# A fused LRU and mixture-of-experts layer: more expert tiles inside the last attention quad, loads before stores, third parts on VectorE, and other unused products

## What is computed

```
x = x + LRU(layernorm(x))              # complex linear recurrence, 64 states, input and output matrices, plus D
y = layernorm(x)
h = y + Attention(rmsnorm(y) * ln1)    # 16 heads of size 8, softmax over all 1024 keys
m = rmsnorm(h) * ln2
logits = m @ gate.T                    # 8 experts, the two best, softmax of their logits
out = sum over the 2 experts e: weight_e * (silu(m @ w1[e].T) * (m @ w3[e].T)) @ w2[e].T
result = x + h + out
```

## Time and profile before

| | |
|---|---|
| runs, us | 1098.22, 1098.86, 1103.92; median 1098.86 |
| profiled execution, us | 1099.61, its span 1097.9 |
| busy share of the span | PE 83%, DVE 80%, ACT 64%, POOL 32% |
| mean granted clock of PE | 0.935 |
| opening | 0 to 196.9 us |
| last quad, first tile to last | 881.3 to 918.5 us |
| tiles behind the quad | 922.9 to 1080.6 us |

### The profile page before, as it was taken

One profiled execution on the slowest core, in us unless ns is written; L12 is line 12 of the kernel. 1 busy time (PEld: TensorE's weight loads), 2 busy tenths in 40 slices (PEclk: granted clock), 3 DMA queues, 4 the chain that ended last, 5 costly groups with the idle time before them and its releaser, 6 DMA issues.

```text
span 1097.9 us, 18609 instructions
## 1 busy us (share of the span) xinstructions
PE 909.0 (83%) x5924; PEld 379.2 (35%) x5924; DVE 877.7 (80%) x1585; ACT 698.8 (64%) x1475; POOL 352.1 (32%) x636
## 2 busy tenths in 40 slices
PE   0376754999999999899899999989999888787783
PEld 0254430222222223222222222222332246787772
DVE  4987759899999988889889999888897733674365
ACT  2235530688888887788878888878877765342331
POOL 4001121000000143433522614524465513456563
PEclk9688875999999999999999999999998999898987
DMA  9984445000010110100100010010010111222263
GB/s 320 387 299 111 108 121 137 8 24 8 27 27 8 24 28 11 43 9 28 45 9 23 25 35 23 13 39 22 16 36 9 45 33 41 57 70 71 69 193 110
DMA packets 62943, 74.48 MB, mean 68 GB/s; under 512 B 11264, under 2 KB 41216, under 8 KB 62464
## 3 DMA queue, kind: packets, MB, share of 16 engines
q1 hardware_dynamic: 56048, 63.07, 19.2%
q0 software_dynamic: 4608, 9.58, 2.6%
q10 hardware_dynamic: 2192, 0.66, 0.3%
HBM read 28.09 MB, written 44.79 MB: 66 GB/s over the span
## 4 chain that ended last, share of the span: by engine, by line
PE 59%; DVE 25%; ACT 7%; issue 5%; DMA 2%; another core or an unknown queue 1%; ACTq 1%; DVEq 0%; POOLq 0%; SPq 0%
PE ps L1605 19%; PE ps L1595 14%; DVE smax L1222 12%; PE ps L1546 7%; PE ps L1703 7%; PE ps L1719 3%; ACT prob L987 3%; PE ps L1563 2%; PE ps L1664 2%; DMA wgate<-gate_t 1%; ACTq L867 1%; PE ps L1683 1%; PE ps L1624 1%; ACT zres L900 1%
## 5 line engine op out<-in xcount | busy, mean ns | idle before, releaser
L1222 DVE TENSOR_REDUCE smax<-ps 128x2 f32<-128x1024 f32 x512 | 600.0, 1220 | 57.4 <-PE ps L1546 48.5
L987 ACT ACTIVATE prob<-ps 128x512 f32<-128x512 f32 x1024 | 533.9, 603 | 101.9 <-PE ps L1595 94.2
L1595 PE MATMUL ps<-packs 51*128 51x512 bf16 x1024 | 310.5, 384 | 31.4 <-ACT prob L987 20.1
L1546 PE MATMUL ps<-packs 51*128 51x512 bf16 x1024 | 256.2, 394 | 29.2 <-DVE smax L1222 22.9
L1605 PE MATMUL ps<-prob,vpad 128*32 128x512 f32 x2048 | 275.2, 610 | 0.0
L1595 PEld LDWEIGHTS ps<-packs 51*128 51x128 bf16 x1024 | 78.3, 94 | 296.4 <-ACT prob L987 206.3
L811 POOL DMA_INDIRECT by_token<-wk,vall x80 | 78.4, 980 | 101.8 <-ACT wk L1047 42.6
L1703 PE MATMUL ps<-ws 128*128 128x128 f32 x640 | 96.1, 298 | 14.1 <-issue 7.1
L1703 PEld LDWEIGHTS ps<-ws 128*128 128x128 f32 x640 | 86.9, 211 | 24.1 <-issue 15.2
L540 POOL MEMSET packs<- 3x1024 f32 x32 | 30.2, 945 | 195.4 <-PE ps L1595 194.3
L1546 PEld LDWEIGHTS ps<-packs 51*128 51x128 bf16 x1024 | 53.2, 94 | 110.6 <-DVE smax L1222 88.8
(11 more groups left out here) (282 smaller groups left out, 859.2 us busy)
## 6 DMA issues: line engine op xcount, KB each, us to landing
by_expert_rows<-prob SPq DMA_DIRECT2D x4, 5016.0 KB, 36.8
vall<-by_expert_rows SPq DMA_DIRECT2D x80, 66.0 KB
packs<-k_parts SPq DMA_DIRECT2D x32, 128.0 KB, 2.8
packs<-q_parts SPq DMA_DIRECT2D x64, 64.0 KB, 2.3
packs<-by_token SPq DMA_DIRECT2D x8, 512.0 KB
w<-w_t SPq DMA_DIRECT2D x3, 1024.0 KB, 10.6
q_parts<-front_raw SPq DMA_DIRECT2D x16, 192.0 KB, 3.0
k_parts<-front_raw SPq DMA_DIRECT2D x16, 192.0 KB, 3.2
```

The source lines that it names most:

```text
L987: act.activation(prob[:, v % RING, :], bank(col_bank(pos)), ACT.Exp).then_inc(col_free, 1)
L1222: dve.tensor_reduce(smax[:, half, :, pair, qt, kh], ps[:, first:first + 2, :], AX_X, ALU.max).then_inc(row_free, 1)
L1546: ins = pe.matmul(bank(first + par), qpack[r:r + ROWS, slot, half, pair, qt * P:(qt + 1) * P], kpack[r:r + ROWS, slot, pair, kh * HALF:(kh ...
L1595: pe.matmul(bank(col_bank(pos)), kpack[r:r + ROWS, slot, head // 2, kt * P:(kt + 1) * P], qpack[r:r + ROWS, slot, half, head // 2, :], sta ...
```

## The change

1. The last quad holds sixteen tiles: one in each of groups 6 to 9, two in each of groups 10 to 15 (`TILES_IN`, `tiles_in`), so J0 is 16. 64 tiles follow.
2. `LATE`, `FRONT_AT` and POOL's scatters of late rows are retimed, most by one or two tiles. POOL does two scatters per tile only from J0 + 38 on, not in every third tile.
3. DVE, not POOL, adds `h` of the late blocks to the residual.
4. `COMBINE` is 72, with one combination per tile, not two.
5. SP issues the last two token loads in front of stores 2 to 5.
6. `third_parts` runs on DVE: those of batches 0 and 1 behind `norm_a` of the next batch, those of batch 2 behind `norm_a(3)`, those of batch 3 between the first sixteen maxima and the rest.
7. PE does 8, 2, 2 and 28 unused bf16 products ahead of the wait for `a_ready` in batches 0 to 3, and one behind each of the first sixteen pairs of opening scores. The four unused float32 products go.

```diff
-        G0, J0 = 6, 10
+        TILES_IN = {g: 1 if g < 10 else 2 for g in range(6, 16)}
+        G0, J0 = min(TILES_IN), sum(TILES_IN.values())
+
+        def tiles_in(g):
+            first = sum(n for h, n in TILES_IN.items() if h < g)
+            return range(first, first + TILES_IN.get(g, 0))
...
-            13: ("logits", 6), 15: ("turn_h", 7), 18: ("ranks", 6), 20: ("logits", 7), 25: ("ranks", 7)}.items()}
+            13: ("logits", 6), 15: ("turn_h", 7), 18: ("ranks", 6), 19: ("logits", 7), 24: ("ranks", 7)}.items()}
-        COMBINE = 67
+        COMBINE = 72
...
             for t in range(EARLY):
                 load_y(t)
-                if t >= 3:
-                    store(t - 3)
-            for t in range(EARLY - 3, EARLY):
-                store(t)
+                if t >= 4:
+                    store(t - 4)
             written(GROUPS)
             for t in range(EARLY, BLOCKS):
                 load_y(t)
-            for t in range(EARLY, BLOCKS):
+            for t in range(EARLY - 4, BLOCKS):
                 store(t)
...
-                if j == J0 + 8:
-                    add_h(EARLY)
-                if j == J0 + 13:
-                    add_h(EARLY + 1)
-                if j == J0 + 23:
+                if j == J0 + 22:
                     gp.wait_ge(late_placed, 1)
                     waiting += [(EARLY, n) for n in range(8)]
-                if j == J0 + 30:
+                if j == J0 + 28:
                     gp.wait_ge(late_placed, 2)
                     waiting += [(EARLY + 1, n) for n in range(8)]
                 gp.wait_ge(y_saved, j + 1)
-                for _ in range(2 if j % 3 == 2 or waiting and waiting[0][0] == EARLY + 1 else 1):
+                for _ in range(2 if j > J0 + 37 or waiting and waiting[0][0] == EARLY + 1 else 1):
...
+            def third_parts(b):
+
+                for w in range(2):
+                    dve.wait_ge(mid_ready, b * 2 + w + 1)
+                    dve.tensor_tensor(qk3[:, w, 2, :], rest[:, w, :], qk3[:, w, 1, :],
+                                      ALU.subtract).then_inc(third_ready, 1)
...
                 norm_a(step, b)
+                if b >= 1:
+                    third_parts(b - 1)
                 states(step, b + 1)
...
             norm_a(step, B - 1)
+            third_parts(B - 2)
             split_qk(B - 1)
...
             split_maxima(0, 16, start)
+            third_parts(B - 1)
             maxima(16, PAIRS - 2, 0, opening=True)
...
+                yield
+                dve.tensor_tensor(xacc[:, 4 * t:4 * t + 4, :], xacc[:, 4 * t:4 * t + 4, :], h, ALU.add).then_inc(late_added, 1)
...
-                EARLY: (5, 6, 7, 7, 8, 8, 9, 15, 15, 16, 20, 20, 21),
-                EARLY + 1: (10, 10, 11, 11, 12, 12, 13, 22, 22, 23, 27, 27, 28, 29, 29, 30)}.items()}
+                EARLY: (5, 6, 7, 7, 8, 8, 9, 14, 15, 15, 16, 20, 20, 21),
+                EARLY + 1: (10, 10, 11, 11, 12, 12, 13, 17, 21, 21, 22, 26, 26, 27, 27, 28, 28)}.items()}
...
+            def unused_product(o_bank):
+                pe.matmul(bank(o_bank), ident16[:, :], ident16[:, :].unsqueeze(1).to_broadcast([P, HALF // P, P]),
+                          start=True, stop=True)
...
+                for _ in range((8, 2, 2, 28)[b]):
+                    unused_product(0)
                 pe.wait_ge(a_ready, b * TILES + TILES)
...
                 score_rows(p, 0, 0, opening=True)
+                unused_product(2)
...
-            for _ in range(4):
-                pe.matmul(bank(PV_BANK), ident[:, :], flat13[:, 0:HALF], start=True, stop=True)
...
-                    if q + 1 == QUADS and g >= G0:
-                        pe_tile(g - G0)
+                    for j in tiles_in(g) if q + 1 == QUADS else ():
+                        pe_tile(j)
```

More of the change, by code:

```diff
@@ L247, in build_program @@
         dest_ready = sem("dest_ready")
-        late_sum, late_norm, late_placed = sem("late_sum"), sem("late_norm"), sem("late_placed")
+        late_norm, late_placed = sem("late_norm"), sem("late_placed")
         x_turned, x_saved = sem("x_turned"), sem("x_saved")
@@ L572, in keep_z @@
                           n, z_kept, 1)
-            def third_parts(b):
-                for w in range(2):
-                    gp.wait_ge(mid_ready, b * 2 + w + 1)
-                    gp.tensor_tensor(qk3[:, w, 2, :], rest[:, w, :], qk3[:, w, 1, :],
-                                     ALU.subtract).then_inc(third_ready, 1)
-            for b in range(B - 1):
-                third_parts(b)
             keep_z(B - 1, 0)
@@ L589, in _ @@
             fill_values(1, 1)
-            third_parts(B - 1)
             def refill(q):
@@ L798, in late @@
                 return LATE_POS[name, t] + 1
-            def add_h(t):
-                gp.wait_ge(late_sum, t - EARLY + 1)
-                gp.tensor_tensor(xacc[:, t * 4:t * 4 + 4, :], xacc[:, t * 4:t * 4 + 4, :], zres[:, t * 4:t * 4 + 4, :],
-                                 ALU.add).then_inc(late_added, 1)
             def scatter_y(j):
@@ L1007, in act_quad @@
                         save_x(0)
-                    if q == QUADS - 1 and g >= G0:
-                        j = g - G0
+                    for j in tiles_in(g) if q == QUADS - 1 else ():
                         gate(j)
@@ L1370, in late_front @@
                 dve.sem_inc(fr_free, 1)
-                dve.sem_inc(late_sum, 1)
                 yield
@@ L1467, in _ @@
             for j in range(TILES_T):
-                if j == 10 - G0:
+                if j == tiles_in(10)[0]:
                     finish_o(QUADS - 1, 0, O_LAST + 1, X_BANK, start + count[0])
@@ L1487, in _ @@
                 if j >= COMBINE:
-                    for _ in range(2):
-                        if combined < 4 * EARLY:
-                            combine(combined, start + count[0])
-                            count[0] += 1
-                            combined += 1
+                    combine(combined, start + count[0])
+                    count[0] += 1
+                    combined += 1
             for t in range(combined, B * TILES):
@@ L1576, in _ @@
             first_half(0, first=True)
+            pe.wait_ge(ident_ready, 1)
             product_y(0)
@@ L1779, in _ @@
             pe.wait_ge(lo_ready, 2 * B + 2)
-            pe.wait_ge(ident_ready, 1)
             for p in range(16):
                 score_rows(p, 0, 0, opening=True)
+                unused_product(2)
             turn_maxima(0, 0)
```

## The result

| | before | with the change |
|---|---|---|
| 20 runs each on one chip, median us | 1096.67 | 1101.13 |
| ratio, 95% interval | 1 | 1.0031 [1.0018, 1.0045] |
| profiled execution, us (span) | 1099.61 (1097.9) | 1099.67 (1097.9) |
| mean granted clock | 0.935 | 0.939 |

A forecast was written before the change was run, and what follows sets the result against it. PE and DVE were taken to hold each other most of the time, with no transfer binding. The terms summed to -5.4 us, from the median of 1098.86 to 1093.4 us, with a range of 1085 to 1102.

The forecast's parts named there:

- Items 1 to 4: Opening: third parts on DVE +0.5 and +1.5, float32 products gone -4.9, slow clock +1.5; together -1.4 us.
- Items 1 and 2: Opening, third parts on DVE: +0.5 us for batches 0 to 2, +1.5 for batch 3 between the maxima.
- item 4: Start of quad 0: PE begins at 1.2 GHz without the float32 products, 0 to 3.4 us, +1.5 taken.
- Rival B: Opening: PE's clock holds at 2.4 GHz and the late rows bring no wait, 1087.8 us; chance 0.22.
- Item 5: Last quad: six more tiles at 1.53 us and two more turns of rows, second `down` covered; +10.6 us.
- rival D: Last quad: a group's second tile is not covered and costs about 3.2 us, 1103.4 us; chance 0.12.
- Items 6 and 9: Tail: six fewer tiles at 2.22 us each, -13.3 us; wait for late rows at group 14, +1.5.
- Item 9: Turn of group 14: late rows ready 84.9 us into the tail, PE there at 80.0 to 85.4; +1.5 us.
- Rival C: Tail: PE waits 4.9 us for group 14's late rows, scatters come 2 later, clock falls; 1101.6 us, chance 0.18.
- Item 10: Tail, POOL's order: 50 scatters left take 63 us against 75 for 34 tiles, so POOL is not the bound.
- Item 7: Tail, late sum moved from POOL to DVE: POOL's addition leaves DVE's scaling of late rows, -1.3 us.
- Item 8: Tail, combining: sixteen combinations leave the tiles, -2.5 us, and land in DVE's wait at the end, +1.0.

The follow-up runs named there:

- one_tile: The changed kernel with one tile, as before, in each of the last quad's groups 6 to 15: 0.9988 of the kernel before.
- best_ten: The changed kernel with one tile per group, POOL's old rule and the old opening: 0.9970 of the kernel before, 1094.64 us beside 1097.74.
- open_again: The kernel before with only the opening of the change, run once more for a narrower interval: 1.0015 of the kernel before.
- open_only: The kernel before with only the opening of the change: 1.0001 of the kernel before.
- late_again: The changed kernel with POOL scattering the late rows in one go, on a chip of the slower kind: 1.0043 of the kernel before.
- pool_rule: The changed kernel with POOL's old rule, two scatters in every third tile: 0.9985 of the kernel before.

## Why the prediction was wrong

- **Items 1 to 4, opening: -1.4 forecast, 0 to +2 measured.** Items 1 and 2 were right: slow sums gone, first scores at 164.24, third parts +1.8 between the maxima (+1.5 forecast). The mis-sized term is item 4: 0 to 3.4 with 1.5 taken, 3.2 measured (3.3 us earlier at the first column score, 0.1 at the sixth group's value products). Rival B, that the clock holds, is out: unused products between the pairs kept PE busy and left it at 1.2 GHz.
- **Item 5: +10.6, measured +11.6.** Right in kind: the second `down` is covered (rival D is out), at 2.05 us per double group, not 1.53.
- **Items 6 and 9, the step that failed.** I gave back 2.22 us for each tile taken from the tail, as if the tail's length were tiles times pace, and took 1.5 us for the wait at group 14: -11.8 together. Up to group 14 the tail is a chain from the last turn of `oT` through the late blocks and POOL's scatters, and the tiles only fill it. The wait is 5.69 us on A and 7.76 on B, and six tiles fewer gave 6.4 us there (`one_tile` beside the change), against 11.6 paid. Item 9 had the chain's length nearly right, rows ready 84.9 us behind the tail's first tile where the turn comes at 83.7. It had PE wrong, which was there at 78.0 (83.7 less the wait), not at 80.0 to 85.4. The stage table hides this: the whole stretch is 15.9 us shorter, more than the 13.1 forecast, because the other parts gave 9.5 us (101.5 us behind the last turn of `oT` before, 92.1 in `one_tile`) where I had 1.3. Of these 9.5, 4.9 are a late completion in the trace of before that `one_tile` doesn't have; the rest is not taken apart.
- **Rival C** had this wait at 4.9 and the time at 1101.6, and deserved more than 0.18. That its time fits so well is in part luck: its late scatters of 2 us didn't come (the turn was 1.2 us sooner than item 9 reckoned), and it had nothing for the opening or for the tiles behind group 14.
- **Item 10, the other failure.** I counted POOL's scatters against the time of the tiles (63 us in 75) and called it not the bound. The count was right and the rule was not looked at: one scatter per save, and none while PE waits, piles up outputs. On B POOL is the bound of the end, and putting the late scatters in one go took away 11 us, as much as the whole loss of 10.4 there; on A the rule costs 0 to 5 us, and without it the six tiles are no loss that can be measured.
- **Item 7.** Not measured alone. PE's wait behind the scaled late rows is 0.85 us (959.50), where before had 2.53, and `best_ten` holds this item.
- **Item 8: -2.5 and +1.0.** The tiles behind group 14 took +3.5 and the end +2.4. Whether fewer combinations freed the tiles stays open: that stretch holds 7.4 us of late completions in the trace of the change and none in that of before, and POOL's rule acts there too. But the combinations of before would be worse with sixteen tiles (+4.3 us on B): they must not meet loads that POOL has not made ready. What fewer combinations give for sure is this safety.
- **The sum.** With 3.2 for item 4, 5.7 for item 9, nothing for the tiles behind group 14 and +2.4 for the end, my sum goes from -5.4 to +4.4; +3.4 and +4.8 were measured. That is a sum made after the fact. It leaves out the unforecast gain up to group 14 and the late completions.

## What to carry to other kernels

Before work is moved out of a stage, ask whether that stage is a sum of its steps or a chain that the steps only fill: take the anchor at its start and the thing it waits for, and time that distance by itself. A queue that serves one item per event of another engine stands still with that engine; count its backlog at the wait that you forecast, not its mean load. And work that lets an engine start sooner is worth only what the engine still gains some groups later, since the clock it starts with counts too. Last, read the price of one part beside the others: here six tiles lost 5 to 6 us beside one rule of POOL and nothing beside another.

## What the runs showed of the hardware

- The same kernel takes 1097 to 1100 us on several chips and 1057 on one other. From the first value product of quad 5 to that of the last quad, the change takes 450.8 us on A and 439.4 on B (410.89 to 861.64, 410.64 to 850.06); behind group 14 to the last `down` 61.6 and 40.7.
- On A ACT and DVE see completions of PE late, by 2 to 8 us, often by 4.2; I found nothing in the records of PE, the DMA queues or the clock that shows why. Between one trace and the next of the same tail those over 1.9 us sum to 4.9 us (before), 11.2 (`open_again`) and 17.7 (`open_only`, profiled at 1105.16), so that one trace of a tail on A is not to be read to a few us. Most fall into runs of five or more of POOL's indirect scatters (26.7 of 29.5 us in `late_again`), though not all (8.6 of 14.3 in `pool_rule`); with pauses between them one trace has 2.8, and on B a run of 59 scatters does nothing of the kind. Whether the scatters are the cause, what differs between the chips, and what the way to PE's completions would be, stays open.
- PE, busy for 17.76 of 18 us, stayed at 1.2 GHz, as the stretch of the change from 164 to 182 above shows. The Trainium skill, TensorE: Matmul & The Clock Gate, section "What's actually happening", says that "activity releases the throttle"; this trace doesn't agree for that stretch, and the measurement decides. The stretch from 197 to 206, the first groups of quad 0, still runs at 0.65.
